# One core, four transformer blocks: VectorE's quantising part of a step in the second attention is moved to the step's end

## The chip, the cores and the metric

The kernel runs on one core of a Trainium2 chip. The metric is the device time of one execution in microseconds (us); it comes from the median of three executions. Five engines each run their own instruction stream in order and meet only at semaphores: TensorE (PE, with its weight loads PEld), VectorE (DVE), ScalarE (ACT), GpSimd (POOL) and SyncE (SP), which issues the DMAs.

## The reference

The input X is 4 sequences of 256 tokens of width 512. Four blocks follow one another, each as `x = layernorm(x + block(x))`:

1. a latent attention with 32 heads,
2. a feed-forward layer whose 4-bit (GPTQ) weights are decoded,
3. an attention with 32 heads, done twice with the same queries (keys and values of 8 shared heads, and 32 "latent" keys and values), both results projected back and added: this is "the second attention",
4. a feed-forward layer whose weights are first rounded to the 16-level NF4 code, per block of 64 weights:

```python
def nf4_quant_dequant(w):
    flat = w.reshape(-1, BLOCKSIZE)                     # BLOCKSIZE = 64
    absmax = jnp.max(jnp.abs(flat), axis=1, keepdims=True)
    normalized = flat / jnp.where(absmax == 0, 1.0, absmax)
    bounds = (NF4_CODE[:-1] + NF4_CODE[1:]) * 0.5
    idx = jnp.searchsorted(bounds, normalized)
    return (NF4_CODE[idx] * absmax).reshape(shape)
```

The rounding of block 4 needs only the weights. The kernel does it during block 3, on VectorE and GpSimd, and parks the result in DRAM (`coded_w`).

## The kernel before, in words

`l1_attention_block` (from line 823) is the second attention. Every product is three fp32r matmuls (`product`, lines 63 to 65: high by high, low by high, high by low), so each operand exists as a high and a low half; ScalarE makes the high half by a copy, VectorE or GpSimd the low half by a subtraction.

The work runs in 8 groups of 16 **steps**; step n has j = n // 4 (the head in the group) and b = n % 4 (the sequence). A step computes, for one head and one sequence, both attentions. Group 0 and group 7 are written out with small differences, groups 1 to 6 are a loop. Each engine's order is written by hand. For step n:

- **PE** (line 1307 on): `scores(n)`; `apply(n-2)` (probabilities times values); `turn(n-1)` (transposes of the probabilities); `project` for the next head (unit "A": one in steps with b = 0 and b = 1, two small ones at b = 2, none at b = 3); two `output` units (the projection of the head before). In steps 1 and 9 the value units V and LV follow (`values`: six in step 1, four in step 9). Units go through a ring of three PSUM banks; a bank is free again when DVE has read it.
- **ACT** (line 1153 on): `out_high(n-2)`; `exps(n)` (L1122); `probs_high(n-1)` (L1138, tile a_pt_hi); `shares_applied(n)` (L1130); `rope_high` (L1109); in steps 1 and 9 `plain_high` (L1114).
- **DVE** (line 1483 on): `peaks(n)` (four masked maxima L1403 and the shift L1409); `out_low(n-2)` (L1427); `codes(n)`, the quantising part; `probs_low(n-1)` (L1419, tile a_pt_lo: the low probabilities); `shares(n)` (L1414, one reciprocal, for which `shares_applied(n)` waits); `rotate` for each A unit of the step (L1384 to L1390, 4 instructions); two `add_output` (L1366, the additions to X, which free ring banks); in steps 1 and 9 `plain_low` (L1394).
- **POOL** (line 1089 on): `code_sums(n)` (L1081), then `rope_low` of the step's A units (L1033), then `pieces(n)`: the splitting of the weights that arrived (L1023 high, L1025 low). The piece of the next head's query weights (a_wq) is split in steps with b = 3 and used by `project` in the step after; the piece WKV is split in step 10.
- **SP**: loads the weight pieces in turn into two raw buffers, and once per head, in `codes`, waits for DVE's `code_end`, stores nf_acc to coded_w, waits for DVE's nf_unit and loads the next nf_raw.

The quantising part `codes(n)` on DVE is, for b = 0, `code_end` of the head before (L1437), `code_start` (L1447 to L1455: block maxima, inverse, scaled weights nf_unit) and three terms; for b = 1, 2, 3 four terms each (`code_terms`, L1467, one compare-and-multiply of 128x512, for the last head of a group 128x576). POOL adds each term to nf_acc in `code_sums`, which is the first thing in its step:

```python
for n in range(STEPS):
    j, b = divmod(n, BATCH)
    code_sums(j, b)
    if j < PER - 1 or not last:
        for i in MADE[b]:
            rope_low(("A", j, i), roped, roped_place)
    pieces(n)
```

In `code_sums` the first add of a head also waits until the store of the head before has landed.

Of the kernel before, what the change touches and what calls it, by code (L numbers as in the profile page):

```python
# [42 lines left out]
def wait(eng, sem, value):  # L43

    if isinstance(value, int) and value <= 0:
        return
    eng.wait_ge(sem, value)


def hold(eng, passed, *waits):  # L50


    for sem, value in waits:
        wait(eng, sem, value)
    if any(not isinstance(value, int) for _, value in waits):
        eng.sem_inc(passed, 1)
# [766 lines left out]
def l1_attention_block(nc, X, XT, LQ, ident, banks, w_q, w_lk, w_kv, w_lv, w_o, cos_d, sin_d, mask_d, w_nf, coded_w):  # L823
# [8 lines left out]
    with ExitStack() as ctx:  # L832
# [527 lines left out]
        def _(dve):  # L1360
            dve.wait_ge(tables, 48)

            def add_output(index, bank_index, t):

                wait(dve, unit_done, index + 1)
                dve.tensor_tensor(X[:, t, :], ring[bank_index % 3][:, :], X[:, t, :], ALU.add)\  # L1366
                   .then_inc(ring_free, 1)

            def body(g, first, last):
# [22 lines left out]
                def plain_low(name):  # L1392
                    wait(dve, v_hi, plain[name] + 1)
                    dve.tensor_tensor(plain_cell(name, (V.lo, LV.lo)), plain_bank(name, ring[bank_of[name] % 3]),  # L1394
                                      plain_cell(name, (V.hi, LV.hi)).bitcast(F32), ALU.subtract)\
                       .then_inc(ring_free, 1)

                def peaks(n):


                    hold(dve, passed["dve"], (scored, STEPS * g + n + 1), (turned, STEPS * g + n - 1))
                    for i, (r, p, bank, at, col, keys) in enumerate(calls):
                        ins = dve.tensor_tensor_reduce(  # L1403
                            out=probs[:, n % 2, col:col + keys], in0=bank[:, at:at + keys],
                            in1=mask[:, SEQ - keys:SEQ], scale=1.0, scalar=NEG, op0=ALU.add, op1=ALU.max,
                            accum_out=peak[:, n % 2, i:i + 1])
                    ins.then_inc(peaked, 1)
                    wait(dve, peaked, STEPS * g + n + 1)
                    dve.tensor_scalar(shift[:, n % 2, :], peak[:, n % 2, :], -scale, None, ALU.mult)\  # L1409
                       .then_inc(shifted, 1)  # L1410

                def shares(n):
                    wait(dve, exped, NC * (STEPS * g + n + 1))
                    dve.reciprocal(share[:, n % 2, :], total[:, n % 2, :]).then_inc(shared, 1)  # L1414

                def probs_low(n):
                    wait(dve, pt_hi, STEPS * g + n + 1)
                    for p, bank in enumerate((TA, TB)):
                        ins = dve.tensor_tensor(PT.lo[:, p, :], bank[:, 0:3 * P],  # L1419
                                                PT.hi[:, p, :].bitcast(F32), ALU.subtract)  # L1420
                    ins.then_inc(pt_lo, 1)

                def out_low(n):
                    b = n % BATCH
                    at = slice(b * SEQ, (b + 1) * SEQ)
                    wait(dve, ot_hi, STEPS * g + n + 1)
                    dve.tensor_tensor(OT.lo[:, :, at], AV[:, :].rearrange("p (a s) -> p a s", a=NP),  # L1427
                                      OT.hi[:, :, at].bitcast(F32), ALU.subtract).then_inc(ot_lo, 1)

                def code_end(j):  # L1430

                    _, n = code_cols(j % PER)
                    q = PER * g + j
                    blocks = nf_acc[:, 0:n].rearrange("p (a c) -> p a c", c=BLK)
                    wide = nf_top[:, j % 2, 0:n // BLK].unsqueeze(2).to_broadcast([P, n // BLK, BLK])
                    dve.wait_ge(nf_added, 14 * (q + 1))
                    dve.scalar_tensor_tensor(out=blocks, in0=blocks, scalar=-1.0, in1=wide, op0=ALU.add,  # L1437
                                             op1=ALU.mult).then_inc(nf_coded, 1)

                def code_start(j):  # L1440

                    _, n = code_cols(j)
                    q, m = PER * g + j, n // BLK
                    split_ = lambda x: x[:, 0:n].rearrange("p (a c) -> p a c", c=BLK)
                    top = nf_top[:, j % 2, 0:m]
                    dve.wait_ge(nf_landed, 16 * (q + 1))
                    dve.tensor_reduce(top, split_(nf_raw), mybir.AxisListType.X, ALU.max,  # L1447
                                      apply_absolute_value=True).then_inc(nf_measured, 1)
                    dve.wait_ge(nf_measured, 3 * q + 1)
                    dve.scalar_tensor_tensor(out=nf_safe[:, 0:m], in0=top, scalar=0.0, in1=top, op0=ALU.is_equal,  # L1450
                                             op1=ALU.add).then_inc(nf_measured, 1)
                    dve.wait_ge(nf_measured, 3 * q + 2)
                    dve.reciprocal(nf_inv[:, 0:m], nf_safe[:, 0:m]).then_inc(nf_measured, 1)
                    dve.wait_ge(nf_measured, 3 * q + 3)
                    dve.tensor_tensor(split_(nf_unit), split_(nf_raw),  # L1455
                                      nf_inv[:, 0:m].unsqueeze(2).to_broadcast([P, m, BLK]), ALU.mult)\
                       .then_inc(nf_unit_done, 1)

                def code_terms(j, b):

                    _, n = code_cols(j)
                    q = PER * g + j
                    wait(dve, nf_added, 14 * q + (0, 2, 6, 10)[b])
                    if b == 0:
                        dve.wait_ge(nf_unit_done, q + 1)
                    for i, k in enumerate(CODE_TERMS[b]):
                        dve.tensor_scalar(nf_term[:, i, 0:n], nf_unit[:, 0:n], BOUNDS[k], JUMPS[k], ALU.is_gt,  # L1467
                                          ALU.mult).then_inc(nf_terms, 1)

                def codes(n):  # L1470
                    j, b = divmod(n, BATCH)
                    if b == 0:
                        if not (first and j == 0):
                            code_end(j - 1)
                        code_start(j)
                    code_terms(j, b)
# [6 lines left out]
                for n in range(STEPS):  # L1483
                    j, b = divmod(n, BATCH)
                    outs = [("O", j, 2 * b), ("O", j, 2 * b + 1)] if (j or not first) else []
                    if n == 0:
                        if not first:
                            out_low(-2)
                            probs_low(-1)
                            for o in outs:  # L1490
                                add_output(number[o], bank_of[o], o[2])
                        rotate(("A", 0, 0))
                        peaks(0)
                        codes(0)
                        shares(0)
                        continue
                    peaks(n)
                    if not (first and n < 2):
                        out_low(n - 2)
                    codes(n)  # L1500
                    probs_low(n - 1)
                    shares(n)
                    if j < PER - 1 or not last:
                        for i in MADE[b]:
                            rotate(("A", j, i))
                    for o in outs:
                        add_output(number[o], bank_of[o], o[2])
                    if n == 1:
                        for i in range(2):
                            plain_low(("V", 0, i))  # L1510
                        for i in range(4):
                            plain_low(("LVa", 0, i))
                    if n == 9:
                        for i in range(4):
                            plain_low(("LVb", 0, i))
                if last:
# [4 lines left out]
                    for t in range(TT):  # L1521
                        add_output(TOTAL_UNITS + t, TOTAL_UNITS + t, t)

            groups(dve, body)


# [499 lines left out]
```

## Time and profile before

| | |
|---|---|
| median of 3 executions | 3381.5 us (3379.79 to 3382.22) |
| profiled execution, its own time | 3376.67 us |
| its span, first to last instruction | 3374.9 us |
| mean granted clock of TensorE | 0.833 of 2.4 GHz |
| steps of the second attention | from 1259 us to about 3075 us of the span |
| busy in the span | PE 79%, DVE 71%, PEld 65%, POOL 40%, ACT 37% |

The span is what the profile divides; the profiled execution's time is 1.8 us longer than its span and 4.8 us shorter than the median. Row views: the timeline gives start, duration, engine, line, operation and tiles, how many instructions were merged (x4), and in brackets how long the engine had stood idle and what ended the wait. Weight loads of PE (PEld) overlap its matmuls.

### The profile page before, as it was taken

To read this page: it belongs to the slowest core of one execution; us is meant where nothing else is said; L and a number is where in the kernel's file an instruction comes from. 1 tells how busy PE (TensorE), PEld (TensorE's weight loads), DVE (VectorE), ACT (ScalarE), POOL (GpSimd) and SP (SyncE) were. 2 spreads that over 40 slices of the span, in tenths; PEclk is the share of its full clock that TensorE was granted. 3 is DMA by queue.
4 is the path that set the end of the run, shared out by engine and by line. 5 is a ranking of instruction groups with operands and counts; after the bars stand their busy time and mean duration, and the time that the engine had idled before them with its cause. 6 is when DMAs were issued, how large, how long until landed. Compare 5 with 4: busy or idle time off the path is not lost. (4 is left out here: it accounts for less than half of the span.)

```text
span 3374.9 us, 44384 instructions
## 1 busy us (share of the span) xinstructions
PE 2665.7 (79%) x13328; PEld 2188.9 (65%) x13328; DVE 2394.4 (71%) x5252; ACT 1254.4 (37%) x3582; POOL 1353.4 (40%) x1020
## 2 busy tenths in 40 slices
PE   6778788787579957877788787788777887877797
PEld 4566666666357746766676676677666766766675
DVE  2667676666764457879878978978798789785345
ACT  1444445455022223434434434334344344344321
POOL 0222222221012125555645646655566466452221
PEclk8677777777569978988898888788888888898899
DMA  1000000000000010101101100101011011002000
GB/s 62 21 24 16 23 20 20 23 20 1 27 1 0 0 46 29 32 32 36 35 17 39 36 29 26 39 29 39 27 35 35 17 39 35 29 20 110 0 0 25
DMA packets 36276, 92.36 MB, mean 27 GB/s; under 512 B 3924, under 2 KB 7128, under 8 KB 34928
## 3 DMA queue, kind: packets, MB, share of 16 engines
q1 hardware_dynamic: 36084, 90.01, 8.3%
q8 instruction: 94, 1.54, 0.2%
q14 instruction: 98, 0.80, 0.1%
HBM read 79.25 MB, written 10.75 MB: 27 GB/s over the span
## 5 line engine op out<-in xcount | busy, mean ns | idle before, releaser
L1081 POOL TENSOR_TENSOR a_nf_acc<-a_nf_acc,a_nf_term 128x512 f32<-128x512 f32 (+1 forms) x416 | 570.3, 1371 | 389.2 <-DVE a_nf_term L1467 335.0
L1467 DVE TENSOR_SCALAR a_nf_term<-a_nf_unit 128x512 f32<-128x512 f32 (+1 forms) x480 | 413.0, 921 | 4.6 <-POOL a_nf_acc L1081 1.2
L63 PE MATMUL bank<-a_wo_hi,a_ot_hi 128*128 128x512 f32 x512 | 225.1, 440 | 196.7 <-DVE a_crossed L1387 196.7
L1130 ACT ACTIVATE a_probs<-a_probs,a_share 128x128 f32<-128x128 f32 (+1 forms) x512 | 191.2, 444 | 373.1 <-DVE a_share L1414 373.1
L444 POOL TENSOR_TENSOR a_q_lo<-a_straight,a_q_hi 128x512 fp32r<-128x512 f32 x64 | 81.7, 1276 | 552.5 <-ACT a_q_hi L473 552.5
L63 PEld LDWEIGHTS bank<-a_wo_hi,a_ot_hi 128*128 128x128 f32 x512 | 106.3, 208 | 230.8 <-DVE a_crossed L1387 209.5
L1122 ACT ACTIVATE a_probs<-a_probs,a_shift 128x128 f32<-128x128 f32 (+1 forms) x512 | 226.2, 444 | 72.2 <-DVE a_shift L1409 71.8
L1575 POOL TENSOR_TENSOR f_w_lo<-WGU,f_w_hi 128x512 fp32r<-128x512 f32 x48 | 60.7, 1290 | 450.7 <-ACT f_w_hi L1593 450.7
L65 PE MATMUL bank<-a_wo_hi,a_ot_lo 128*128 128x512 f32 x512 | 215.4, 421 | 0.0
L64 PE MATMUL bank<-a_wo_lo,a_ot_hi 128*128 128x512 f32 x512 | 215.2, 420 | 0.0
L1629 DVE TENSOR_TENSOR f_hidden<-bank,f_act_gate 128x512 f32<-128x512 f32 x48 | 33.2, 692 | 244.2 <-ACT f_act_gate L1602 244.2
L487 ACT ACTIVATE a_probs<-a_probs,a_shift 128x128 f32<-128x128 f32 (+1 forms) x256 | 114.4, 447 | 225.9 <-DVE a_shift L721 225.9
L619 PE MATMUL bank<-ident,a_probs 128*128 128x128 f32 x384 | 92.3, 364 | 128.0 <-ACT a_probs L495 128.0
L63 PE MATMUL bank<-XT_hi,a_wq_hi 128*128 128x512 f32 x256 | 130.6, 510 | 59.4 <-POOL a_wq_lo L1025 59.4
L1366 DVE TENSOR_TENSOR X<-bank,X 128x512 f32<-128x512 f32 x256 | 163.2, 676 | 6.0 <-PE bank L65 6.0
L63 PE MATMUL bank<-XT_hi,f_w_hi 128*128 128x512 f32 x384 | 151.1, 394 | 9.8 <-POOL f_w_lo L1575 9.8
L619 PEld LDWEIGHTS bank<-ident,a_probs 128*128 128x128 f32 x384 | 51.5, 175 | 165.0 <-ACT a_probs L495 141.2
L63 PE MATMUL bank<-a_wlv_hi,XT_hi 128*128 128x256 f32 x512 | 146.1, 285 | 11.5 <-DVE a_crossed L1387 11.5
L1403 DVE CUSTOM_DVE_ANT_0 a_probs<-bank,a_mask 128x128 f32<-128x128 f32 (+1 forms) x512 | 151.5, 350 | 3.5 <-PE bank L65 2.0
L64 PE MATMUL bank<-XT_lo,f_w_hi 128*128 128x512 f32 x384 | 150.8, 393 | 0.0
L65 PE MATMUL bank<-XT_hi,f_w_lo 128*128 128x512 f32 x384 | 150.6, 392 | 0.0
L1033 POOL TENSOR_TENSOR a_kk_lo<-a_straight,a_kk_hi 128x512 fp32r<-128x512 f32 x80 | 102.9, 1286 | 105.9 <-ACT a_kk_hi L1109 105.9
(256 smaller groups left out, 8930.6 us busy)
## 6 DMA issues: line engine op xcount, KB each, us to landing
a_raw<-in_l_o SPq DMA_DIRECT2D x48, 512.0 KB, 3.6
n_codes<-coded_w SPq DMA_DIRECT2D x8, 1056.0 KB, 12.4
a_raw<-in_l_q SPq DMA_DIRECT2D x32, 256.0 KB, 2.6
a_raw<-in_l_lv SPq DMA_DIRECT2D x16, 512.0 KB, 3.5
a_nf_raw<-in_w_nf SPq DMA_DIRECT2D x24, 256.0 KB, 3.5
coded_w<-a_nf_acc SPq DMA_DIRECT2D x24, 256.0 KB, 4.1
a_raw<-in_l_n SPq DMA_DIRECT2D x16, 256.0 KB, 2.7
a_raw<-in_l_kv SPq DMA_DIRECT2D x8, 512.0 KB, 4.1
```

The source lines that it names most:

```text
L63: pe.matmul(out, lh, rh, start=first, stop=False)
L64: pe.matmul(out, lh, rl, start=False, stop=False)
L65: return pe.matmul(out, ll, rh, start=False, stop=last)
L487: act.activation(cell, cell, ACT.Exp, bias=shift[:, n % 2, i:i + 1], scale=scale, accum_out=total[:, n % 2, i:i + 1]).then_inc(exped, 1)
L619: last_ = pe.transpose(TA[:, i * P:(i + 1) * P], probs[:, n % 2, i * P:(i + 1) * P], ident[:, :])
L1033: pool.tensor_tensor(to.lo, straight[:, place[name] % 2, :], to.hi.bitcast(F32), ALU.subtract)\
L1081: pool.tensor_tensor(nf_acc[:, 0:n], before, nf_term[:, i, 0:n], ALU.add).then_inc(nf_added, 1)
L1122: act.activation(cell, cell, ACT.Exp, bias=shift[:, n % 2, i:i + 1], scale=scale, accum_out=total[:, n % 2, i:i + 1]).then_inc(exped, 1)
L1130: ins = act.activation(cell, cell, ACT.Copy, scale=share[:, n % 2, i:i + 1])
L1366: dve.tensor_tensor(X[:, t, :], ring[bank_index % 3][:, :], X[:, t, :], ALU.add)\
L1403: ins = dve.tensor_tensor_reduce(out=probs[:, n % 2, col:col + keys], in0=bank[:, at:at + keys], in1=mask[:, SEQ - keys:SEQ], scale=1.0, s ...
L1467: dve.tensor_scalar(nf_term[:, i, 0:n], nf_unit[:, 0:n], BOUNDS[k], JUMPS[k], ALU.is_gt, ALU.mult).then_inc(nf_terms, 1)
```

## The change

In a step of the second attention `codes(n)` no longer stands ahead of `probs_low(n-1)` and `shares(n)`, but behind the last `add_output` (in steps 1 and 9 ahead of `plain_low`). In step 0, which has `probs_low` and the additions ahead of its peaks, `shares(0)` and `codes(0)` change places. No instruction is added or removed, and the streams of the other engines are as they were.

```diff
@@ -1491,13 +1491,12 @@
                                 add_output(number[o], bank_of[o], o[2])
                         rotate(("A", 0, 0))
                         peaks(0)
+                        shares(0)
                         codes(0)
-                        shares(0)
                         continue
                     peaks(n)
                     if not (first and n < 2):
                         out_low(n - 2)
-                    codes(n)
                     probs_low(n - 1)
                     shares(n)
                     if j < PER - 1 or not last:
@@ -1505,6 +1504,7 @@
                             rotate(("A", j, i))
                     for o in outs:
                         add_output(number[o], bank_of[o], o[2])
+                    codes(n)
                     if n == 1:
                         for i in range(2):
                             plain_low(("V", 0, i))
```

## Rows read from the trace of the kernel before

**Rows 1.** The page, busy time of each engine over the whole span.
```profile
PE 2665.7 (79%) x13328; PEld 2188.9 (65%) x13328; DVE 2394.4 (71%) x5252; ACT 1254.4 (37%) x3582; POOL 1353.4 (40%) x1020
```
**Rows 2.** The second attention as one stretch: busy PE, PEld, DVE, ACT, POOL, clock, DMA.
```profile
1259.00:3075.00 1816.00, 1444.19 (x7932) 1238.12 (x7932) 1503.05 (x3178) 727.81 (x2137) 1051.21 (x768) 0.87 0.10 31
```
**Rows 3.** What DVE waited for in it: us in total, times, longest.
```profile
DVE a_lv_lo L1394 <- ACT a_lv_hi L1114: 133.1, 64, 2.2
DVE a_v_lo L1394 <- ACT a_v_hi L1114: 70.1, 16, 4.7
```
**Rows 4.** Timeline of DVE, step 3 of a middle group and the next step's start.
```profile
1996.33 0.28 DVE L1403 CUSTOM_DVE_ANT_0 a_probs<-bank,a_mask 128x128 f32<-128x128 f32 x1
...
1998.84 2.53 DVE L1467 TENSOR_SCALAR a_nf_term<-a_nf_unit 128x512 f32<-128x512 f32 x4
2001.28 1.01 DVE L1419 TENSOR_TENSOR a_pt_lo<-bank,a_pt_hi 128x384 fp32r<-128x384 f32 x2
...
2003.47 0.28 DVE L1403 CUSTOM_DVE_ANT_0 a_probs<-bank,a_mask 128x128 f32<-128x128 f32 x1
```
**Rows 5.** Timeline of ACT in the same step.
```profile
1999.84 0.85 ACT L1138 ACTIVATE a_pt_hi<-bank 128x384 fp32r<-128x384 f32 x2
2002.41 1.50 ACT L1130 ACTIVATE a_probs<-a_probs,a_share 128x128 f32<-128x128 f32 x4 [1.71 <-DVE a_share L1414]
```
**Rows 6.** The same pair, DVE's terms and ACT's a_pt_hi, in step 1.
```profile
1950.74 3.58 DVE L1467 TENSOR_SCALAR a_nf_term<-a_nf_unit 128x512 f32<-128x512 f32 x4
...
1951.73 0.85 ACT L1138 ACTIVATE a_pt_hi<-bank 128x384 fp32r<-128x384 f32 x2
```
**Rows 7.** The same pair in step 15 of that group.
```profile
2156.08 4.06 DVE L1467 TENSOR_SCALAR a_nf_term<-a_nf_unit 128x576 f32<-128x576 f32 x4
...
2157.09 0.85 ACT L1138 ACTIVATE a_pt_hi<-bank 128x384 fp32r<-128x384 f32 x2
```
**Rows 8.** Timeline of POOL over steps 3 and 4: sums, split of a_wq, next sums.
```profile
1999.51 1.57 POOL L1081 TENSOR_TENSOR a_nf_acc<-a_nf_acc,a_nf_term 128x512 f32<-128x512 f32 x1 [2.26 <-DVE a_nf_term L1467]
...
2004.19 1.27 POOL L1081 TENSOR_TENSOR a_nf_acc<-a_nf_acc,a_nf_term 128x512 f32<-128x512 f32 x1 [0.18 <-POOL a_nf_acc L1081]
...
2006.13 1.67 POOL L1025 TENSOR_TENSOR a_wq_lo<-a_raw,a_wq_hi 128x512 fp32r<-128x512 f32 x1
2012.74 1.28 POOL L1081 TENSOR_TENSOR a_nf_acc<-a_nf_term 128x512 f32<-128x512 f32 x1 [4.95 <-DMA coded_w<-a_nf_acc]
```
**Rows 9.** Timeline of PE in step 4: the projection begins.
```profile
2007.85 0.79 PE L63 MATMUL bank<-XT_hi,a_wq_hi 128*128 128x512 f32 x1 [3.02 <-POOL a_wq_lo L1025]
```
**Rows 10.** Timeline of DVE in step 4: code_end, terms, rotation; then step 5 begins.
```profile
2006.00 0.68 DVE L1437 SCALAR_TENSOR_TENSOR a_nf_acc<-a_nf_acc,a_nf_top 128x512 f32<-128x512 f32 x1
...
2008.89 1.10 DVE L1467 TENSOR_SCALAR a_nf_term<-a_nf_unit 128x512 f32<-128x512 f32 x3
...
2013.38 0.69 DVE L1384 TENSOR_TENSOR a_straight<-bank,a_cos 128x512 f32<-128x512 f32 x1 [2.37 <-PE bank L65]
...
2017.62 0.29 DVE L1403 CUSTOM_DVE_ANT_0 a_probs<-bank,a_mask 128x128 f32<-128x128 f32 x1 [0.22 <-PE bank L65]
```
**Rows 11.** That projection as a stretch; columns as in rows 2.
```profile
2007.85:2013.40 5.55, 5.55 (x13) 4.39 (x14) 3.03 (x9) 1.76 (x5) 0.66 (x1) 0.50 0.62 189
```
**Rows 12.** Step 1: PE begins the first value unit, DVE gets it.
```profile
1958.68 0.22 PE L63 MATMUL bank<-a_wkv_hi,XT_hi 128*128 128x128 f32 x1
...
1964.82 0.69 DVE L1394 TENSOR_TENSOR a_v_lo<-bank,a_v_hi 128x512 fp32r<-128x512 f32 x1 [4.64 <-ACT a_v_hi L1114]
```
**Rows 13.** Step 14: DVE's terms while POOL splits weights.
```profile
2137.83 7.50 DVE L1467 TENSOR_SCALAR a_nf_term<-a_nf_unit 128x576 f32<-128x576 f32 x4
...
2141.03 2.42 POOL L1025 TENSOR_TENSOR a_wlv_lo<-a_raw,a_wlv_hi 128x1024 fp32r<-128x1024 f32 x1
```
**Rows 14.** All terms of the kernel: duration in ns, min, median, max.
```profile
L1467 DVE TENSOR_SCALAR a_nf_term<-a_nf_unit x480: 411/446/2615, 1262.2 to 3068.2; 128x512 f32<-128x512 f32 x120, 128x576 f32<-128x576 f32 x40
```
**Rows 15.** The page, the group of all terms: busy us, mean ns.
```profile
L1467 DVE TENSOR_SCALAR a_nf_term<-a_nf_unit 128x512 f32<-128x512 f32 (+1 forms) x480 | 413.0, 921 | 4.6 <-POOL a_nf_acc L1081 1.2
```

## The prediction

> **What bounds the kernel now.** I read the page first: no engine fills the span, and VectorE's 71% is an average over unlike stages [rows 1]. So I cut out the second attention, the only stage the change touches: 1816 us, in which DVE is busy 1503 (83%), PE 1444 (80%, at a mean clock of 0.87), POOL 1051 and ACT 728 [rows 2]. Next the waits. Of DVE's 313 us without work, 203 lie in the value units of steps 1 and 9, where it waits for the high halves that ACT makes behind PE [rows 3]. What is left, 110 us, is under 1 us for each of the 128 steps. The reader should see that outside the value units DVE runs without a break: it sets the pace there, and PE does in the value units. Idle time added to DVE outside them is added to the kernel.
>
> Then the timeline of one step. In step 3 DVE starts its peaks at 1996.33 and the four terms at 1998.84; they take 2.53, and a_pt_lo follows at 2001.28 without a wait [rows 4]. ACT finishes a_pt_hi, which a_pt_lo needs, at 1999.84 + 0.85 = 2000.69 [rows 5]. The terms therefore cover the time in which ACT does the exponentials and a_pt_hi.
>
> **The change, part by part.** Everything is summed for one middle group of 16 steps, in the profiled execution.
>
> *The gap that opens.* With the terms gone from their place, DVE stands from the end of out_low (where the terms began) until a_pt_hi: 2000.69 - 1998.84 = 1.85 us in step 3 [rows 4, 5], 1951.73 + 0.85 - 1950.74 = 1.84 in step 1 [rows 6], 2157.09 + 0.85 - 2156.08 = 1.86 in step 15 [rows 7]. ACT's order is unchanged and its chain starts from DVE's shift, so nothing brings a_pt_hi nearer. Step 0 has no a_pt_lo there, but its reciprocal waits for the same exponentials; I take the same value. 16 x 1.85 = **+29.6**. Bounds: 0, if ACT were always ahead, and 2.5 a step (40) if the shift itself is late.
>
> *What shares and the rotation gain.* The reciprocal now comes 0.7 us sooner behind the peaks (2.53 out, 1.85 in), so ACT's scaling, which waits 1.71 for it today [rows 5], starts sooner, and so do the transposes. Outside steps with b = 0 nobody who sets the pace waits for these: **0**, covered by DVE's own queue, since the terms still have to be done before the next peaks. If PE were the late one, this would be worth at most that 0.7 a step.
>
> *Cover at the new place.* In steps 1 and 9 the terms now stand where DVE would wait for the value units: 4.64 us in step 1, from PE's first value matmul at 1958.68 to 1964.82 [rows 12]. The terms there cost 3.58 today [rows 6] and in step 9 about the 2.53 of rows 4: together **-6.1**. The start of the value units hangs on the rotation before them, hardly moved: steps 0 and 1 lose two gaps, 3.7, and gain 3.58. Bounds 0 and -7.2 (twice 3.58).
>
> *The queue of POOL, at b = 0.* code_sums is first in POOL's step, and the split of the next head's query weights is queued behind it. From the first term of step 3 to its first add 0.67 us pass [rows 4, 8]; the split ends at 2006.13 + 1.67 = 2007.80 [rows 8], where PE, idle for 3.02, begins the projection [rows 9], which takes 5.5 us at clock 0.50 [rows 11], and DVE rotates at 2013.38 after waiting 2.37 [rows 10]. From first term to rotation: 14.54 us, a chain over POOL and PE that the change does not shorten. Today DVE fills all but 2.37 of it. In the new order only these lie within it: the terms 2.53, peaks, shift and out_low 2.51 (1998.84 - 1996.33), the gap 1.85, a_pt_lo and the reciprocal 1.1, in all 8.0. The two additions have gone before it and code_end, nf_unit and three terms (2006.00 to 2009.91, 3.9 us) behind it. DVE waits 14.5 - 8.0 = 6.5, which is 4.1 more, at the steps 4, 8 and 12: **+12.3**. Before step 12 POOL also splits WKV (step 10, queued behind the sums and the rotations' low halves) and comes late to the sums of step 11; by the low part alone of a piece of 1024 columns, 2.42 us [rows 13], **+2.4**. Bounds for both: 0 if POOL's chain turns out short, and another 2.4 for each of the three if a longer split stands in the way.
>
> *SP's and POOL's other queues.* SP's store of nf_acc and its load of nf_raw wait for code_end and nf_unit, now one rotation and two additions later; the next weight pieces stand behind them in SP's queue. The first add of a head waits for that store: today it starts at 2012.74, 6.1 us after code_end's end at 2006.68 [rows 8, 10]. In the new order this falls into step 5's first half, while its result is used by DVE only at that step's end, and the weight pieces are needed a step or more later: **0**. If that cover is gone, 6.1 us of waiting less what has passed by then, perhaps 3, at four steps a group: +12 as an upper bound.
>
> *The pair of engines that disturb each other.* A term takes 411 ns at the least, 446 in the median and 2615 at most [rows 14], with a mean of 921 [rows 15]. The long ones lie beside POOL's work: 7.50 us for four in step 14 while POOL splits weights [rows 13], 1.10 for three in step 4 while POOL waits for the store [rows 10]. At a step's end POOL has mostly finished and waits for the very terms, as in step 3 (0.63 a term) or step 1 (0.90) [rows 4, 6]. Today, three of 15 terms of a head at 0.37 leave (15 x 0.921 - 1.1) / 12 = 1.06 for the others. I take 0.86, near the upper of the two rows since a fifth of the terms is wider: 40 terms outside steps 1 and 9, 40 x 0.2 = **-8**. Bounds: 0, and 40 x (1.06 - 0.446) = -25. Against it, POOL's four adds now fall beside the next peaks, and the shift, which opens ACT's chain, can wait for an add; an estimate from rows 8, half of a 1.3 us add in every third step: **+3**, between 0 and 10.
>
> Here the Trainium skill has a rule, in SBUF — State Buffer, "Who interferes with whom": a two-port VectorE instruction and a GpSimd instruction exclude one another, and whoever comes second stands still for the whole of the other. The rows agree in kind (7.50 against 1.10). Followed to its end, terms issued while POOL has nothing would all cost the bare time, and the change would pay; the last rival prices that from the rows.
>
> **Sum.** 29.6 - 6.1 + 12.3 + 2.4 - 8 + 3 = +33.2 us a group. Eight groups: +266; the last has no projection in step 12, -6.5: +259. Against the profiled execution, 3376.67 + 259 = 3636; the median of the runs lies 4.8 us above that execution, so **3640 us**, 7.6% slower.
>
> **The rivals.**
> *B, the chain at b = 0 is absorbed* (the projection runs at the full clock, or POOL is quicker): the +12.3 and +2.4 fall away, 8 x 14.7 - 6.5 = 111 us, leaving 3529. For it: 5.5 us at clock 0.50 would be 2.8 at full clock. Against it: PE has been idle for 3 us there already and will be for longer. Chance 0.10.
> *C, the disturbance stays*: terms cost the same at the new place (+8 a group) and the shift and rotations suffer twice what I allowed for the next adds (+3): 8 x 11 = 88, 3728. For it: POOL is busy for 1051 of the 1816 us [rows 2], wherever the terms stand. Against it: where POOL's earlier work was done it stood waiting for the very terms, 2.26 us in step 3 [rows 8]. Chance 0.18. Of the clock a rule speaks the same way: TensorE: Matmul & The Clock Gate, "HAM oscillation", says that waits between bursts of matmuls send the array back to half clock each time. The row of the projection agrees (0.50 behind 3.02 us of idling); by the rule more projections than that one would take 5.5 us, most of them behind DVE's own work.
> *D, faster: the change pays through the disturbance.* Its place is L1467: were all 480 terms to fall to the median, 413.0 - 480 x 0.446 = 199 us would go [rows 14, 15], and 8 x 6.1 = 49 under the value units, 248 in all. Against that stand the gaps, 8 x 29.6 = 237. If the chain at b = 0 costs nothing too, 3381.5 - 11 = 3370. It decides at a gap of 248 / 128 = 1.94 us: above that, even this perfect case is slower. Against it: POOL's adds come straight behind the terms that they use, so step 3's own four, with POOL idle before, still took 0.63 each. Chance 0.04.
> *E, nothing moves*: DVE's idle time merely changes place, or the order had no hold on the pace, 3381. Against it: 83% busy, with no waits outside the value units. Chance 0.02. That the change doesn't do what it says is part of this; an engine follows its written order.
>
> **How the numbers follow.** The forecast has 0.66, with 3580 to 3700 as its own range (8 groups, 7 us a group each way, from the bounds of the lock and the gap). Slower by over 0.2% (7 us, about what a measurement of this kernel tells from no change): 0.66 + 0.10 + 0.18 = 0.94; faster 0.04; same 0.02. The range 3540 to 3710 leaves out most of B, half of C, and D and E, some 0.2.
>
> **What would show it.** In the changed kernel's waits DVE a_pt_lo L1419 <- ACT a_pt_hi, not among the leading rows today [rows 3], should be a leading row with about 112 waits of some 1.8 us; DVE a_straight <- PE bank should grow from waits of 2.4 to about 6.5 at three steps a group; the terms' mean should fall below 0.921; POOL should wait longer and oftener for a_nf_term; the waits for a_v_hi should lose about 3 us in each step 1. A step with b = 3 should last 9 us for 7.1 today. I am wrong if the gap is there and PE or POOL was the pace-setter after all, seen as a stage hardly longer than 1816 us, or if the terms become so cheap that they outweigh it.

## The result and the profile after

The changed kernel takes 3639.4 us (median of 4, 3634.1 to 3644.0) against 3381.9 before (median of 4): ratio 1.076, 95% interval 1.074 to 1.078, 258 us slower. The forecast was 3640. The profiled execution took 3634.1 us, its span is 3632.1, TensorE's mean clock 0.816.

The second attention, from its first step on, as in [rows 2]:

```profile
1259.00:3335.00 2076.00, 1544.84 (x7934) 1332.86 (x7933) 1416.20 (x3169) 728.03 (x2132) 1040.16 (x768) 0.84 0.09 27
```

It is longer by about 260 us, the whole difference. DVE was busy 1503 us of 1816 and is now busy 1416 of 2076: 87 us less work and some 350 us more idling. What DVE waited for in it, as in [rows 3]:

```profile
DVE a_pt_lo L1419 <- ACT a_pt_hi L1138: 243.2, 120, 2.7
DVE a_lv_lo L1394 <- ACT a_lv_hi L1114: 137.4, 60, 4.3
DVE a_straight L1384 <- PE bank L65: 105.6, 23, 6.3
DVE a_v_lo L1394 <- ACT a_v_hi L1114: 105.1, 15, 9.5
```

The first row is new. The third was 40 us in 21 waits, and the fourth 70 us; that it grew was not foreseen. These rows and 15.4 us for the reciprocals of the eight steps 0 (a_share waiting for ACT's a_probs) are the new idling: 243 + 65 + 4 + 35 + 15 is 362 us, less some 10 saved at out_low. Timeline of DVE, steps 3 and 4 of the same middle group, as in [rows 4, 10]:

```profile
2101.19 0.28 DVE L1403 CUSTOM_DVE_ANT_0 a_probs<-bank,a_mask 128x128 f32<-128x128 f32 x1
...
2105.26 1.02 DVE L1419 TENSOR_TENSOR a_pt_lo<-bank,a_pt_hi 128x384 fp32r<-128x384 f32 x2 [2.09 <-ACT a_pt_hi L1138]
...
2107.46 2.72 DVE L1467 TENSOR_SCALAR a_nf_term<-a_nf_unit 128x512 f32<-128x512 f32 x4
2110.45 0.29 DVE L1403 CUSTOM_DVE_ANT_0 a_probs<-bank,a_mask 128x128 f32<-128x128 f32 x1 [0.27 <-PE bank L65]
...
2120.68 0.69 DVE L1384 TENSOR_TENSOR a_straight<-bank,a_cos 128x512 f32<-128x512 f32 x1 [3.78 <-PE bank L65]
```

The gap of 2.09 us stands where the terms were; step 3 lasts 9.26 us instead of 7.14; at b = 0 DVE waits 3.78 for the rotation instead of 2.37, and code_end, nf_unit and three terms come after it. Timelines of POOL and then of PE in the same stretch, as in [rows 8, 9]:

```profile
2114.92 1.26 POOL L1025 TENSOR_TENSOR a_wq_lo<-a_raw,a_wq_hi 128x512 fp32r<-128x512 f32 x1
```
```profile
2116.23 0.79 PE L63 MATMUL bank<-XT_hi,a_wq_hi 128*128 128x512 f32 x1 [2.92 <-POOL a_wq_lo L1025]
```

The terms as a group on the changed kernel's page, as in [rows 15]: 71 us cheaper, and POOL now stands waiting for them for 943 us in the stage (418 before).

```profile
L1467 DVE TENSOR_SCALAR a_nf_term<-a_nf_unit 128x512 f32<-128x512 f32 (+1 forms) x480 | 341.6, 773 | 3.3
```

I took the length of every step from the timeline, from one start of L1409 to the next. In us, for the group of the rows:

| step | 0 | 1 | 2 | 3 | 4 | 5 | 6 | 7 | 8 | 9 | 10 | 11 | 12 | 13 | 14 | 15 | sum |
|---|---|---|---|---|---|---|---|---|---|---|---|---|---|---|---|---|---|
| before | 5.0 | 34.4 | 13.9 | 7.1 | 14.2 | 12.3 | 15.2 | 6.7 | 13.9 | 21.1 | 14.0 | 8.9 | 14.2 | 11.5 | 18.1 | 21.7 | 232.2 |
| after | 7.1 | 40.7 | 15.0 | 9.3 | 17.7 | 11.7 | 15.6 | 9.2 | 17.9 | 21.9 | 15.0 | 11.9 | 19.1 | 11.8 | 18.7 | 23.1 | 265.6 |

The group is 33.4 us longer (forecast 33.2), but not where I had put it: step 1 alone carries 6.2, of which I had foreseen nothing. From the timelines of PE and then of DVE of the changed kernel, the start of the value units of step 1 and DVE's wait behind them:

```profile
2052.78 0.33 PE L63 MATMUL bank<-a_wkv_hi,XT_hi 128*128 128x128 f32 x1 [2.59 <-DVE a_crossed L1387]
```
```profile
2072.74 0.69 DVE L1394 TENSOR_TENSOR a_v_lo<-bank,a_v_hi 128x512 fp32r<-128x512 f32 x1 [9.55 <-ACT a_v_hi L1114]
```

The stretch of these two units, columns as in [rows 2], first in the changed kernel, then in the kernel before:

```profile
2057.00:2072.80 15.80, 15.80 (x75) 15.80 (x75) 0.83 (x3) 1.19 (x2) 8.38 (x6) 0.50 0.10 34
```
```profile
1958.70:1969.60 10.90, 10.90 (x99) 10.90 (x98) 2.17 (x4) 1.29 (x3) 4.67 (x3) 1.00 0.14 50
```

PE is busy without a pause in both, at 2.4 GHz before and at 1.2 GHz after. Before, it went from the outputs into the values without idling; after, it had idled for 2.59 us. The granted clock fell to 0.50 only at 2054.4, inside the first unit, and was 1.00 again from 2074.9 on, in the LV units. This became the first question of the experiments.

### The profile page after: what moved, and what is told of

The parts are those of the page before. It is cut to its first block and busy times, and to the rows that moved or that the text cites. A ratio compares the mean times of both kernels' runs of the same rounds, so it can differ in the third digit from the quotient of the medians.

```text
span 3632.1 us, 44384 instructions
## 1 busy us (share of the span) xinstructions
PE 2764.4 (76%) x13328; PEld 2281.6 (63%) x13328; DVE 2308.6 (64%) x5252; ACT 1257.1 (35%) x3582; POOL 1342.1 (37%) x1020
## 5 line engine op out<-in xcount | busy, mean ns | idle before, releaser
L1467 DVE TENSOR_SCALAR a_nf_term<-a_nf_unit 128x512 f32<-128x512 f32 (+1 forms) x480 | 341.6, 773 | 3.3
L63 PE MATMUL bank<-a_wo_hi,a_ot_hi 128*128 128x512 f32 x512 | 217.3, 424 | 164.6 <-DVE a_crossed L1387 164.6
L1419 DVE TENSOR_TENSOR a_pt_lo<-bank,a_pt_hi 128x384 fp32r<-128x384 f32 x256 | 130.9, 553 | 243.7 <-ACT a_pt_hi L1138 243.2
L63 PE MATMUL bank<-a_kk_hi,a_q_hi 128*128 128x256 f32 (+1 forms) x256 | 110.5, 432 | 168.1 <-POOL a_kk_lo L1033 136.9
L1629 DVE TENSOR_TENSOR f_hidden<-bank,f_act_gate 128x512 f32<-128x512 f32 x48 | 33.2, 692 | 244.7 <-ACT f_act_gate L1602 244.7
L1081 POOL TENSOR_TENSOR a_nf_acc<-a_nf_term 128x512 f32<-128x512 f32 (+1 forms) x32 | 43.3, 1353 | 386.1 <-DVE a_nf_term L1467 351.3
L63 PEld LDWEIGHTS bank<-a_kk_hi,a_q_hi 128*128 128x128 f32 x256 | 61.9, 242 | 188.7 <-issue 104.1
L63 PE MATMUL bank<-a_wlv_hi,XT_hi 128*128 128x256 f32 x512 | 156.2, 305 | 28.2 <-DVE a_crossed L1387 28.2
L1384 DVE TENSOR_TENSOR a_straight<-bank,a_cos 128x512 f32<-128x512 f32 x144 | 97.0, 674 | 121.9 <-PE bank L65 118.8
## 6 DMA issues: line engine op xcount, KB each, us to landing
n_codes<-coded_w SPq DMA_DIRECT2D x8, 1056.0 KB, 12.3
```

The source lines that it names most:

```text
L63: pe.matmul(out, lh, rh, start=first, stop=False)
L1081: pool.tensor_tensor(nf_acc[:, 0:n], before, nf_term[:, i, 0:n], ALU.add).then_inc(nf_added, 1)
L1384: dve.tensor_tensor(two(row), two(bank[:, :]), wide(cos[:, :]), ALU.mult)
L1419: ins = dve.tensor_tensor(PT.lo[:, p, :], bank[:, 0:3 * P], PT.hi[:, p, :].bitcast(F32), ALU.subtract)
```

## The experiments

GAP is the uncovered wait for ACT; QUEUE is POOL's chain at b = 0; CLOCK is the slow values of step 1. The kernel before, run beside each set of experiments, had medians from 3375.0 to 3381.9 us, so a difference between two sets carries some 5 us; the ratios don't.

**1. Step 0 put back** (changed kernel).
```diff
                         peaks(0)
-                        shares(0)
                         codes(0)
+                        shares(0)
```


> The changed kernel, with step 0 alone put back (codes(0) ahead of shares(0)). In the changed kernel PE stood idle for 2.59 us ahead of the first value unit of step 1, and its clock fell to 0.50 within the two V units (10.2 us for the second, 5.4 before); step 1 lasts 40.6 us against 34.4. Theory (idling before the values): the earlier reciprocal of step 0 lets PE finish its transposes, projection and outputs of step 1 some 3 us sooner, so it idles before the values; with the old order it does not, the V units run at full clock, and step 1 falls to about 35 us: 7 groups x 5 to 6 us, some 3600 us in all. Rival (the clock falls for some other reason, such as the lower load of the whole stage): step 1 stays at 40 us and the time within 5 us of 3639.

Measured: 3571.9 us, ratio 1.058 (1.056 to 1.060), 68 us under the changed kernel; expected was some 40. Step 0 falls by 2.0 and step 1 by 7.6 us, to 33.0. DVE's wait for the V units in this kernel's profile is half of what it was:

```profile
DVE a_v_lo L1394 <- ACT a_v_hi L1114: 51.2, 15, 4.7
```

and the seven us of its value units that I looked at (columns as in [rows 2]) are at 2.4 GHz again:

```profile
2030.00:2037.00 7.00, 7.00 (x65) 7.00 (x65) 3.89 (x7) 0.83 (x2) 5.11 (x4) 1.00 0.00 0
```

The slow values belong to the exchange in step 0. I had the size too small: step 1 with the new place and fast values is shorter than before, 33.0 against 34.4.

**2 and 3. POOL's sums cut short**, in the old order (2) and in the new (3). 13 of a head's 14 additions are one column wide, so the coded weights of the last block are incomplete.
```diff
-                        before = nf_term[:, 0, 0:n] if k == 1 else nf_acc[:, 0:n]
+                        m = n if k == 1 else 1
+                        before = nf_term[:, 0, 0:n] if k == 1 else nf_acc[:, 0:m]
...
-                        pool.tensor_tensor(nf_acc[:, 0:n], before, nf_term[:, i, 0:n], ALU.add).then_inc(nf_added, 1)
+                        pool.tensor_tensor(nf_acc[:, 0:m], before, nf_term[:, i, 0:m], ALU.add).then_inc(nf_added, 1)
```


> The kernel before, but 13 of the 14 additions of a head on POOL are one column wide instead of 512 or 576 (the sums are left out, so the coded weights are not the reference's; terms, order and semaphores stay). This takes away both the disturbance of the terms and the length of POOL's queue at b = 0. Theory: terms fall to about 0.45 us, the wait of 2.4 us at the rotation of steps 4, 8, 12 goes: 3376 - 8 x (25 + 7) = about 3130 us. To be compared with the next kernel.

> The changed kernel with the same short additions on POOL (the same sums left out). Theory (the uncovered wait for ACT is the main cost): bare terms of 4 x 0.45 = 1.8 us would just fill the gap of 1.85, so the new order costs about 1.8 to 1.85 us in 14 steps of 16 even with POOL out of the way, and the values of step 1 still run slow: 200 to 250 us above the kernel with short sums in the old order. Rival (POOL's queue at b = 0 and the disturbance are the main cost): under 100 us above it. Waits for a_pt_hi stay near 240 us in the trace by the first, and by both the wait at the rotation of b = 0 falls under 1 us.

Measured: 3190.9 and 3394.2 us, 203 us apart: with POOL's sums cut in both, the new order still costs four fifths of its price. DVE's wait for a_pt_hi, from the waits of kernel 2 (old order) and then of kernel 3 (new order; lines are one further down in both):

```profile
DVE a_pt_lo L1420 <- ACT a_pt_hi L1139: 30.5, 60, 0.8
```
```profile
DVE a_pt_lo L1420 <- ACT a_pt_hi L1139: 246.9, 121, 2.7
```

The first row says that bare terms, 1.8 us for four, are just too short to cover ACT. Kernel 3 also shows CLOCK by itself: step 1 lasts 31.0 us in groups 2, 4, 5 and 7 and 40.6 in 1, 3 and 6, with nothing between. A slow pair of V units costs 9.6 us. PE had idled for 1.41 to 1.66 us ahead of the short ones, for 1.68 to 1.72 ahead of the long ones. The wait at the rotation did not quite go (49.6 us in 22 waits, and 21.2 in 21 in kernel 2), and kernel 2 came 60 us above my estimate. So the 203 us are not GAP alone: three slow pairs are 29 of them in the profiled execution, and in groups 1 to 6 more than half of the difference (15 of 28 us a group) lies in steps 4, 8 and 12, where the quantising part now stands behind the rotation.

**4. The split ahead of the sums at b = 3**, new order.
```diff
                     j, b = divmod(n, BATCH)
+                    if b == 3:
+                        pieces(n)
                     code_sums(j, b)
...
-                    pieces(n)
+                    if b != 3:
+                        pieces(n)
```


> The changed kernel, but in steps with b = 3 POOL splits the next head's query weights ahead of its four additions instead of behind them. Theory (the wait at b = 0 comes from that queue): the chain loses the four additions, 5.8 us, and DVE's waits of 3.8, 3.9 and 6.1 us at the rotations of steps 4, 8 and 12 go, 13.8 us a group at most: between 3535 and 3580 us. Rival (the queue only looks guilty, PE or DVE would be late anyway): within 15 us of 3639.

Measured: 3546.9 us, ratio 1.051 (1.049 to 1.054), 92.6 us under the changed kernel. The row a_straight <- PE is gone from DVE's waits; step 4 falls from 17.7 to 12.8 us, step 3 rises from 9.3 to 10.4. CLOCK is still there: step 1 takes 31.0 us in group 1 and 40.6 to 42.2 in groups 2 to 7. QUEUE is real and worth 92.6 us, or 4.0 for each of 23 head transitions.

**5, 6, 7. What helps the kernel before**: the new place in steps 1 and 9 alone (5), the split of experiment 4 alone in the old order (6), both (7).
```diff
                     peaks(n)
                     if not (first and n < 2):
                         out_low(n - 2)
-                    codes(n)
+                    moved = n in (1, 9)
+                    if not moved:
+                        codes(n)
...
                         add_output(number[o], bank_of[o], o[2])
+                    if moved:
+                        codes(n)
```


> The kernel before, with the new place of codes in steps 1 and 9 alone. Theory (the terms are covered there by the waits for the value units, and with the old step 0 PE does not idle before them): step 1 falls by some 1.4 us as it did between the kernel before and the changed kernel with step 0 put back (34.4 to 33.0), step 9 moves by less than 1 us: 3365 to 3378 us, 0.1 to 0.5% faster. Rival (any use of the new place opens the gap of 1.85 us and costs it): 16 x 1.85 = 30 us slower, 3410.

> The kernel before, with POOL's split of the next query weights ahead of its additions in steps with b = 3. Theory (the queue on POOL also made the 2.2 to 2.4 us waits at the rotations of steps 4, 8, 12 of the kernel before): these 23 waits go, 23 x 2.3 = 53 us: 3315 to 3350. Rival (DVE has no slack to give, or the additions that now come later disturb its terms as much): 3370 to 3385.

> The kernel before with both: split ahead of the additions at b = 3, and the new place of codes in steps 1 and 9 alone. By the theories above the two are independent and add up: 3300 to 3345, faster than both kernels of the case. Rival: PE, projecting earlier, idles before the value units of step 1 and loses 9.6 us a group there (the difference between the two lengths that step 1 takes, 31.0 and 40.6 us): 3375 to 3400.

Measured: 3370.6 us, ratio 0.9974 (0.9956 to 0.9993); 3350.8, ratio 0.9907 (0.9881 to 0.9932); 3326.8, ratio 0.985 (0.983 to 0.988). The first and the last lie in their ranges, the second just outside its own (3315 to 3350): it gained 27 us, half of the 53 that the theory named, although DVE's waits for a_straight went as it said (40.2 us in the kernel before, 4.9 in kernel 6). So under the value units the new place does no harm and gains a little; the waits for a_straight in the old order had QUEUE as their cause too; and both together make a version 1.5% faster than the kernel before. Whether the two simply add up is not shown: 7 and 27 us were measured alone and 51 together, and the intervals just allow 34 in its place. In the profiled execution of kernel 6 step 1 of group 1 took 42.9 us, of groups 2 to 7 33.2 to 34.4; its time of 3366.0 us lies 15 over that kernel's median, of which one slow pair of V units would be 9.6. The gains of 5 lie near what a measurement can tell.

**8. The new place at steps 4, 8, 12 alone** (as 5, with `moved = b == 0`).

> The kernel before, with the new place of codes in steps 4, 8 and 12 alone (b = 0). Theory (the rotation there has its time set by POOL's queue and PE, so what stood ahead of it for nothing now stands behind it): code_end, nf_unit and three terms, 3.9 us, are added to each of 23 steps: +90 us, some 3470. Rival (only the gap counts): 23 x 1.85 = 43 us, some 3424.

Measured: 3487.8 us, ratio 1.031 (1.028 to 1.034): +110, over both figures. The sum comes near the theory, but not in the way that it says. In groups 1 to 6 steps 4, 8 and 12 are longer by 1.7, 2.2 and 2.1 us, not by 3.9: the work does stand behind the rotation, but the rotation comes sooner (8.4 us behind the step's first peak in step 4, and 9.9 before), as the projection takes 4.4 us for 5.5. The larger part, 3.0, 3.4 and 1.8 us, lies in the steps behind them: their terms, in their old early place, wait for sums that were started late, and then fall beside POOL's next splits. One slow pair of V units (group 7, 43.7 us for step 1) is some 9 us more in the profiled execution. DVE's waits of kernel 8, then its timeline in step 5 of the middle group, where the terms took 4.14 before:

```profile
DVE a_nf_term L1467 <- POOL a_nf_acc L1081: 22.8, 25, 1.2
```
```profile
2069.20 6.55 DVE L1467 TENSOR_SCALAR a_nf_term<-a_nf_unit 128x512 f32<-128x512 f32 x4 [0.88 <-POOL a_nf_acc L1081]
```

**9. Step 0 put back and the split first**, new order (1 and 4 together).

> The changed kernel with both undoings so far: step 0 in its old order, and POOL's split of the query weights ahead of its additions at b = 3. Theory (three parts that add up: idling before the values, POOL's queue at b = 0, and the uncovered wait for ACT): one gave -68 us, the other -92, so 3639 - 160 = 3480 +- 15 us, which still is 100 us over the kernel before, by the gap alone. Rival (the two overlap, since either lets PE run closer to DVE): over 3510.

Measured: 3472.8 us, ratio 1.029 (1.026 to 1.031). The parts add up: 67.6 + 92.6 = 160, measured 167. In all of its groups step 1 is in its short form. What is left over the kernel before is 98 us. The fairer measure of GAP less its savings is kernel 6, which has the same order on POOL and the same step 0: kernel 9 lies 122 us above it (by the two ratios 130). The wait for a_pt_hi is still 242 us, so about half of it is made up elsewhere: the terms are 62 us cheaper than in kernel 6 (373.6 and 435.7 on the two pages), and the waits for the value units 34 us shorter.

**10. ScalarE's order exchanged**, new order.
```diff
-                    exps(n)
                     probs_high(n - 1)
+                    exps(n)
                     shares_applied(n)
```


> The changed kernel, but ScalarE makes the high half of the probabilities of step n-1 ahead of the exponentials of step n, not behind them. Theory (DVE's 243 us of waiting for a_pt_hi are ACT's exponentials standing ahead of it, 1.8 us a step): a_pt_hi is then ready about when out_low ends, DVE does a_pt_lo (1.0 us) while ACT does the exponentials, and the wait moves to the reciprocal at 0.1 to 1.0 us a step: 100 to 200 us fewer, 3440 to 3540. Rival (the wait is set by PE's transposes, so that its place in ACT's order does not matter): within 25 us of 3639.

Measured: 3538.8 us, ratio 1.047 (1.041 to 1.052), 101 us under the changed kernel. The gap has gone from a_pt_lo, and a quarter of it has moved on to the reciprocal, as DVE's waits of kernel 10 show:

```profile
DVE a_share L1414 <- ACT a_probs L1122: 77.3, 128, 1.9
...
DVE a_pt_lo L1419 <- ACT a_pt_hi L1138: 15.0, 38, 0.9
```

ACT's place of a_pt_hi behind the exponentials made the gap. Of 228 us taken from that wait 62 came back at the reciprocal (77.3 for 15.4), 15 at the rotations, whose time QUEUE sets (waits for a_straight 120.4 us for 105.6, the longest 9.3), and 58 in the terms, which are as dear again as before the change (399.9 us on the page, and 341.6 in the changed kernel).

**11. The new place at b = 1 and 2 alone**, without steps 1 and 9 (`moved = b in (1, 2) and n not in (1, 9)`).

> The kernel before, with the new place of codes in steps with b = 1 and b = 2 alone, without steps 1 and 9: six steps a group (2, 5, 6, 10, 13, 14), away from POOL's queue at b = 0 and from step 0. By the prediction's terms: 6 x 1.85 less 24 terms x 0.2 = 6.3 us a group, +50 us, some 3428. By the step lengths of the changed kernel (step 2 +1.0, 5 -0.6, 6 +0.5, 10 +1.0, 13 +0.3, 14 +0.6): +2.8 a group, +22 us, some 3400.

Measured: 3516.1 us, ratio 1.042 (1.039 to 1.044): +141, far outside both figures. The moved steps themselves did as forecast from the table (step 2 +1.0, 5 -0.3, 6 +0.4, 10 +1.0, 13 +0.3, 14 +0.6). The loss is in the unmoved steps behind them. Timeline of DVE in step 3 of kernel 11:

```profile
2046.10 2.51 DVE L1467 TENSOR_SCALAR a_nf_term<-a_nf_unit 128x512 f32<-128x512 f32 x4
...
2052.72 5.73 DVE L1467 TENSOR_SCALAR a_nf_term<-a_nf_unit 128x512 f32<-128x512 f32 x4 [2.21 <-POOL a_nf_acc L1081]
```

Two sets of terms come too close: DVE is ready for the early ones 4.4 us after it began the late ones, and POOL's four additions need 1.3 to 1.5 us each. DVE waits 2.21 for the term buffers, then its terms, 5.73 for 2.5, meet POOL's instructions. Step 3 takes 12.0 us, longer than in either pure order. So this experiment could not price GAP alone: a mixed order has a cost of its own. It warns of 8, and of 5 less, since values of some 15 us stand behind its moved terms.

**12. The exchange in step 0 alone**, in the kernel before.

> The kernel before, with the exchange of codes(0) and shares(0) in step 0 alone. Theory (an earlier reciprocal lets PE finish early and idle before the value units, whose clock then falls): step 0 +2.0, and step 1 takes its long form (9.6 us more) in most of the groups: +50 to +90 us, 3430 to 3465. Rival (the exchange costs its gap only): 8 x 1.9 = 15 us, 3392; or it shortens step 1 by as much as it lengthens step 0: 3377.

Measured: 3455.9 us, ratio 1.024 (1.022 to 1.027). Step 0 +2.0, step 1 in its long form in all of groups 1 to 7 (44.0 to 45.1 us for 34.4). PE idled for 3.1 to 6.0 us ahead of the values in these groups; one of them in the timeline of PE of kernel 12:

```profile
1978.42 0.47 PE L63 MATMUL bank<-a_wkv_hi,XT_hi 128*128 128x128 f32 x1 [5.01 <-DVE a_crossed L1387]
```

Two lines exchanged, with no work added, cost 2.4%. With experiment 1 this shows from both sides that the exchange brings the slow values.

**What PE did ahead of the values.** For all 8 groups of all 14 profiles, the idle time of PE ahead of the first value matmul of step 1, and the granted clock at the end of the V units behind it:

| PE idle ahead, us | starts | values at 2.4 GHz | values at 1.2 GHz |
|---|---|---|---|
| 0 to 0.19 | 69 | 69 | 0 |
| 0.85 to 1.68 | 20 | 12 | 8 |
| 1.72 to 6.02 | 23 | 0 | 23 |

In the middle row the idle time does not decide: the clock fell in kernel 6, group 1 (1.39 us), in kernel 3, group 6 (1.68 us), and in six groups of kernel 10 behind only 0.92 to 1.30 us, while it held in the twelve others, most of them behind 1.38 to 1.66 us. In the changed kernel the idle time is 1.82 to 2.89 us in groups 1 to 7. In the 6 us ahead of every start that fell, the mean clock had been 0.89 or more, so a low clock was not merely carried over. That the idling is the cause, and not something that goes with it, was not varied by itself; that the exchange in step 0 brings both is shown.

## Why the prediction came out right, point by point

- *DVE sets the pace outside the values.* Right: its new idling shows in the time.
- *The gap*, 1.85 us in 16 steps. Right in place; the size was a little low: 243.2 us in 120 waits is 2.03 each. Experiment 10 shows ACT's exponentials as the cause. Its price with QUEUE and CLOCK away, less what the new place saves, is the 122 us between kernels 6 and 9; my own terms for that (gap, cover and disturbance, 18.5 a group) make 148.
- *Step 0 and the reciprocal*, "nobody who sets the pace waits for these: 0". This was the step that failed. The earlier reciprocal of step 0 lets PE finish its transposes, projection and outputs early; it then idles for DVE's rotation, and the V units behind it run at 1.2 GHz. Steps 0 and 1 were to cancel (+3.7 - 3.6) and measure +2.0 + 6.2, 8.3 us unrounded. With fast values they would be about 1.4 us shorter than before: +2.0, and 31.0 us for 34.4 (experiment 3, where the sums are cut too, and group 1 of experiment 4, where they are whole). Rival C stands beside the clock rule of the Trainium skill (TensorE: Matmul & The Clock Gate, "HAM oscillation"): waits between bursts send the array back to half clock. The trace agrees, but at the values, where I had not applied it, and not at further projections; and there the clock fell each time only behind waits of 1.72 us or more, and behind shorter ones in 8 of 20 starts.
- *Cover under the values.* Right in kind, too large in size. Experiment 5 has it alone: by my terms 8 × (6.1 - 3.7) = 19 us faster, measured 7. DVE's waits in the value units fell by 33 us (203 to 171), where 49 were forecast.
- *POOL's queue at b = 0*, +12.3 +2.4. The mechanism was right (experiments 4 and 6), the term too large: I expected waits of 6.5 us and they are 3.8, 3.9 and 6.1. Between the first term of step 3 and the rotation there are 13.2 us, not 14.5, because the projection's last five of twelve matmuls already run at 2.4 GHz; and 3.5 us from peaks to the end of out_low (2110.45 to 2113.99) where I had put 2.5, since the tiny shift, beside POOL's work, takes 1.15 us, and out_low waits 0.47 for ACT. The WKV split did make step 12 the worst.
- *SP's and POOL's other queues*, 0. Right for the uniform new order. Experiments 8 and 11 show what lies behind it when the order is mixed: term buffers and sums that are not done.
- *The disturbance*, -8 +3. The terms fell by 71 us, 9 a group, and by 8 a group outside steps 1 and 9, as forecast, but not where I had them: all of it is in steps 5, 6 and 13 to 15 (10 us in groups 1 to 6), while in steps 3, 7 and 11 they cost 2 us more. The +3 was wrong in sign: the shifts take 35 us in all and took 53. Where POOL was late the terms were as dear as ever. Timelines of DVE and then of POOL in step 11 of the changed kernel:

```profile
2225.75 5.71 DVE L1467 TENSOR_SCALAR a_nf_term<-a_nf_unit 128x512 f32<-128x512 f32 x4
```
```profile
2227.34 2.42 POOL L1025 TENSOR_TENSOR a_wkv_lo<-a_raw,a_wkv_hi 128x1024 fp32r<-128x1024 f32 x1
```

Four terms take 5.71 us beside the split of WKV. The Trainium skill's page SBUF — State Buffer, "Who interferes with whom", has the loser stand still for the whole of the other's instruction; these rows agree in kind.
- *The sum.* 33.2 forecast and 33.4 measured a group is better than its terms. By my own terms against the table of steps: steps 0 and 1, +0.1 forecast and +8.3 measured; steps 3, 4, 7, 8, 11, 12, +23.4 (6 × 1.85 + 12.3 + 2.4 - 12 × 0.2) and +20.1 (the two kinds apart: 4, 8 and 12 +20.2 and +12.4; 3, 7 and 11 +3.2 and +7.7); the other eight, +9.7 (8 × 1.85 - 2.5 - 28 × 0.2 + 3) and +5.0. What I missed at the values was made up by 8 us put too high elsewhere. The point was met by errors that cancel; the range is what the working had earned.
- Of the signs named beforehand, one was wrong: the waits for a_v_hi were to shrink and grew from 70 to 105 us.

Open: what decides between 0.85 and 1.68 us of idling, where both outcomes occur; and why the clock, once down, stayed down through more than 15.8 us of unbroken V matmuls while it rose again within the projections and at the LV units. No run varied these.

## What to carry to other kernels

On an in-order engine that sets the pace, off-path work is worth most in the wait that it covers; before you move it, list for each place what would otherwise be waited for there, and which queue on another engine starts from it. Work moved behind a point whose time another engine sets no longer fills the wait there and delays what starts from it: in experiment 8 3.9 us of work came to 4.8 us a time, more than half of it in the next step. And an exchange of two lines in one step of 16 can cost 2.4% through what it does to another engine (12). Where filling and queue are known, look for the queue itself: splitting the needed weights ahead of the sums gave 0.9% on its own.

## What the runs showed of the hardware that I had not expected

- Two V units take 10.8 us (before, 1958.68 to 1969.51) or 19.3 (after, 2052.78 to 2072.07) at the same work. Which it is goes with PE's idling ahead of them: 0.19 us or less in 69 starts, all fast; 1.72 us or more in 23, all slow; both outcomes in the 20 between. Within one execution both forms can occur (experiments 3 and 6), and part of the scatter of these kernels' times is probably that.
- Matmuls of 128 columns with a weight load each stayed at 1.2 GHz for 15.8 us at 100% busy (2057.0 to 2072.8 of the changed kernel), so being busy did not by itself bring the clock back.
- Finishing early went with a slower PE: in experiment 12 PE was done with the outputs 3.3 us behind the shift of step 1 (middle group; 9.5 in the kernel before) and began the values 1.2 us sooner in the step, and step 1 took 10 us more.
